# Banded attention: scores as three rounded passes over split queries and keys, projections three units ahead

## What is computed

```python
q = _apply_rope(proj(Wq, bq)); k = _apply_rope(proj(Wk, bk)); v = proj(Wv, bv)   # 16 heads of 64
qb, kb, vb = (y.reshape(b, NH, nb, W, HD) for y in (q, k, v))                    # blocks of W = 128 tokens
kcat = concat([previous block of kb (zeros for the first), kb])                  # 256 keys per block
scores = einsum('bhnqd,bhnkd->bhnqk', qb, kcat) * scale
scores = where(band and valid, scores, -1e30)
ctx = einsum('bhnqk,bhnkd->bhnqd', softmax(scores), vcat)
x = x + merged(ctx) @ Wo.T + bo
```

## Time and profile before

| | us |
|---|---|
| median of 3 runs (1678.68 to 1683.46) | 1678.73 |
| the profiled execution: its time | 1680.55 |
| the profiled execution: its span | 1678.8 |
| busy in the span: TensorE | 1300.5 |
| VectorE | 1008.7 |
| ScalarE | 918.3 |
| GpSimd | 777.6 |
| window stage, from its first to its last operation, about | 57 to 820 |

### The profile page before, as it was taken

The page is one execution under the profiler, slowest core; times in us unless marked ns, Lnnn a source line. Parts: engine busy times, 40 slices in busy tenths (PEclk is TensorE's granted clock), DMA queues, the critical chain, the costliest instruction groups (busy, mean ns, idle before and its releaser), DMA issues. The chain is left out here.

```text
span 1678.8 us, 35216 instructions
## 1 busy us (share of the span) xinstructions
PE 1300.5 (77%) x9684; PEld 1014.9 (60%) x9684; DVE 1008.7 (60%) x3721; ACT 918.3 (55%) x2325; POOL 777.6 (46%) x797
## 2 busy tenths in 40 slices
PE   0699899999999999999641788925988954187891
PEld 0466666666666666666431688912775844177891
DVE  5565566666666656666684445646885877344553
ACT  1377677777776777777541444513765854044450
POOL 4356566666666666656377244510000007634451
PEclk9799999999999999999855898967999975589896
DMA  5799990000000000000311121130000001121115
GB/s 182 135 208 201 207 204 16 0 1 0 1 0 0 1 0 1 0 1 0 101 51 51 53 65 49 62 103 1 1 2 1 0 2 53 48 60 58 57 56 150
DMA packets 129331, 91.55 MB, mean 55 GB/s; under 512 B 9083, under 2 KB 121998, under 8 KB 128960
## 3 DMA queue, kind: packets, MB, share of 16 engines
q1 hardware_dynamic: 118848, 71.32, 20.1%
q0 software_dynamic: 9216, 16.94, 2.9%
q10 hardware_dynamic: 1152, 2.13, 0.4%
HBM read 30.86 MB, written 61.57 MB: 55 GB/s over the span
## 5 line engine op out<-in xcount | busy, mean ns | idle before, releaser
L666 DVE CUSTOM_DVE_ANT_0 sc<-ps,mask 128x256 f32<-128x256 f32 x518 | 199.3, 422 | 280.7 <-PE ps L507 279.6
L787 POOL TENSOR_TENSOR rot<-rot,sin 128x512 f32<-128x512 f32 x132 | 184.4, 1397 | 249.8 <-DVE rot L675 249.8
L598 ACT ACTIVATE sc<-sc,mx 128x256 f32<-128x256 f32 x516 | 256.9, 501 | 20.0 <-DVE mx L666 11.7
L422 POOL DMA_INDIRECT xg<-xw,slot x128 | 123.9, 968 | 287.1 <-DVE slot L284 251.7
L919 POOL DMA_INDIRECT yt<-yo,xt x160 | 160.3, 1002 | 204.8 <-DVE yo L1019 175.6
L606 ACT COPY pT<-pt 128x512 f32<-128x512 f32 x257 | 150.6, 586 | 149.4 <-PE pt L517 138.4
L507 PE MATMUL ps<-K,Q 64*128 64x256 f32 x1036 | 185.5, 434 | 1.7 <-DVE mx L666 1.7
L979 ACT ACTIVATE hT<-ph,b 128x256 f32<-128x256 f32 x320 | 125.7, 477 | 87.7 <-PE ph L942 87.7
L517 PE MATMUL pt<-ident,sc 128*128 128x128 f32 x1028 | 169.8, 288 | 0.0
L530 PE MATMUL po<-pT,V 128*64 128x128 f32 x2048 | 169.3, 286 | 0.0
L960 PE MATMUL py<-w2s,hT 128*128 128x128 f32 x1280 | 162.2, 282 | 1.4 <-ACT hT L979 1.4
(11 more groups left out here) (185 smaller groups left out, 2846.3 us busy)
## 6 DMA issues: line engine op xcount, KB each, us to landing
xg<-zeros SPq DMA_DIRECT2D x76, 520.0 KB, 10.0
xt<-xg SPq DMA_DIRECT2D x80, 130.0 KB, 2.1
got<-yt SPq DMA_DIRECT2D x32, 256.0 KB, 5.0
yt<-yo,xt POOLq DMA_INDIRECT x160, 2.2
x<-in_hidden SPq DMA_DIRECT2D x8, 256.0 KB, 8.3
w<-in_w SPq DMA_DIRECT2D x1, 2048.0 KB, 9.7
xg<-xw,slot POOLq DMA_INDIRECT x128, 2.3
out_x<-x SPq DMA_DIRECT2D x8, 256.0 KB, 4.2
```

Source lines behind the costliest of these rows:

```text
L422: nc.gpsimd.indirect_dma_start(out=rows, out_offset=bass.IndirectOffsetOnAxis(ap=s.slot[:, r, t:t + 1], axis=0), in_=s.xw[:, r, t, :], in_ ...
L598: nc.scalar.activation(sc[:, b, h, :], sc[:, b, h, :], ACT.Exp, scale=-1.0, bias=mx[:, b, h:h + 1], accum_out=ls[:, c % 2, b, h:h + 1]).th ...
L666: nc.vector.tensor_tensor_reduce(sc[:, b, h, :], ps[:, h, 0:2 * P], (mask0 if b == 0 else mask)[:, :], -float(HD) ** -0.5, 3e38, ALU.add, ...
L787: nc.gpsimd.tensor_tensor(rot[:, which, :], rot[:, which, :], s.sin[:, pos(sb)], ALU.mult).then_inc(S["pool"], 1)
```

## The change

In the window stage, Q and K are each kept as two tiles of rounded fp32 (`Qh`, `Ql`, `Kh`, `Kl`): a high part and what is left. A head's scores are three products, high by high, low K by high Q, high K by low Q, summed in PSUM. GpSimd writes its sum back into `lin` (`q_sum`, `k_sum`); ScalarE rounds it into the high tile (`high`, L629 of the changed kernel), and VectorE subtracts that from `lin` into the low tile (`low`, L703), which now counts `q_rdy` or `k_rdy`. For Q, `high` runs behind `read_pt` in b = 2 and `low` behind the maxima in b = 3; for K both run in b = 0 of the next iteration. Projections are three units ahead (`AHEAD = 3`). The first 128 columns of K are copied twice. The experts' outputs are awaited by pairs of superblocks, with 4 semaphores for 8.

```diff
-    nc.gpsimd.memset(s.K[:, :, :], 0.0)
+    for part in s.K:
+        nc.gpsimd.memset(part[:, :, :].bitcast(F32), 0.0)
...
-            sp.dma_start(got[:, k, r, :], parts[k][:, r, :]).then_inc(s.fetched[i], 16)
+            sp.dma_start(got[:, k, r, :], parts[k][:, r, :]).then_inc(s.fetched[i // 2], 16)
...
-    ch.eng.wait_ge(s.fetched[i], 16 * TOPK * nth)
+    ch.eng.wait_ge(s.fetched[i // 2], 32 * TOPK * nth)
...
-            return u, u + 2, (c + 2) % CHUNKS, (sb if c + 2 < CHUNKS else sb + 1)
+            return u, u + AHEAD, (c + AHEAD) % CHUNKS, (sb if c + AHEAD < CHUNKS else sb + 1)
...
-                    ins = nc.tensor.matmul(ps[:, h, 0:2 * P], Q[r, c % QBUF, b * P:(b + 1) * P],
-                                           K[r, c, b * P:(b + 2) * P], start=True, stop=True)
+                    for n, (i, j) in enumerate(((0, 0), (0, 1), (1, 0))):
+                        ins = nc.tensor.matmul(ps[:, h, 0:2 * P], Q[i][r, c % QBUF, b * P:(b + 1) * P],
+                                               K[j][r, c, b * P:(b + 2) * P], start=(n == 0), stop=(n == 2))
...
+            def high(v, c, which):
+
+                act.wait_ge(S["k_sum" if which else "q_sum"], START + v + 1)
+                if which:
+                    act.wait_ge(S["k_prev"], START + v + 1)
+                to = K[0][:, c, P:] if which else Q[0][:, c % QBUF, :]
+                nc.scalar.copy(to, lin[:, which, :]).then_inc(S["k_high" if which else "q_high"], 1)
...
-            for v in range(2):
+            for v in range(AHEAD):
                 read_q(v, v, v0=(v == 0))
                 read_k(v, v, v0=(v == 0))
+                high(v, v, 0)
+                if v < AHEAD - 1:
+                    high(v, v, 1)
...
                         if b == 0:
+                            high(v - 1, (vc - 1) % CHUNKS, 1)
                             read_q(v, vc)
+                        if b == 2:
+                            high(v, vc, 0)
...
+            def low(v, c, which):
+
+                dve.wait_ge(S["k_high" if which else "q_high"], START + v + 1)
+                to, high = (x[:, c, P:] if which else x[:, c % QBUF, :] for x in ((K if which else Q)[1], (K if which else Q)[0]))
+                nc.vector.tensor_tensor(to, lin[:, which, :], high.bitcast(F32), ALU.subtract).then_inc(
+                    S["k_rdy" if which else "q_rdy"], 1)
...
-            for v in range(2):
+            for v in range(AHEAD):
...
+                low(v, v, 0)
+                if v < AHEAD - 1:
+                    low(v, v, 1)
...
+                        if b == 3:
+                            low(v, vc, 0)
                         if b == 0:
+                            low(v - 1, (vc - 1) % CHUNKS, 1)
                             normalise(u - 1, (c - 1) % CHUNKS)
...
-                if which:
-                    pool.wait_ge(S["k_prev"], START + v + 1)
...
-                nc.gpsimd.tensor_tensor(K[:, c, P:] if which else Q[:, c % QBUF, :], lin[:, which, :],
-                                        rot[:, which, :], ALU.add).then_inc(S["k_rdy" if which else "q_rdy"], 1)
+                nc.gpsimd.tensor_tensor(lin[:, which, :], lin[:, which, :], rot[:, which, :], ALU.add).then_inc(
+                    S["k_sum" if which else "q_sum"], 1)
...
-                nc.gpsimd.tensor_copy(K[:, c, 0:P], K[:, c, SB:]).then_inc(S["k_prev"], 1)
+                nc.gpsimd.tensor_copy(K[0][:, c, 0:P], K[0][:, c, SB:])
+                nc.gpsimd.tensor_copy(K[1][:, c, 0:P], K[1][:, c, SB:]).then_inc(S["k_prev"], 1)
```

More of the change, by code:

```diff
@@ L97 @@
     "norm0": NORM + " xT high",
-    "window": "xs xh xl q_ps k_ps v_ps q_sb k_sb v_sb q_sh k_sh q_cos k_cos q_rdy k_rdy "
+    "window": "xs xh xl q_ps k_ps v_ps q_sb k_sb v_sb q_sh k_sh q_cos k_cos q_sum k_sum q_high k_high q_rdy k_rdy "
               "k_prev v_prev s max p t pt pv rs rb r r_sb norm out res chain pool",
@@ L441, in window_stage @@
         xh, xl = (m.sb(n, [P, 2, SB], F32R) for n in ("xh", "xl"))
-        Q = m.sb("Q", [P, QBUF, SB])
+        Q = [m.sb(n, [P, QBUF, SB], F32R) for n in ("Qh", "Ql")]
         K, V, masks, mask = s.K, s.V, s.masks, s.mask
@@ L459, in window_stage @@
         S = s.signals["window"]
+        AHEAD = 3
         swap = [(w + 16) % 32 for w in range(32)]
@@ L484, in project_q @@
                 else:
-                    pe.wait_ge(S["r_sb"], START + v - 2)
+                    pe.wait_ge(S["r_sb"], START + v - AHEAD)
                 project(s.wqh, s.wql, c, sb).then_inc(S["q_ps"], 1)
@@ L535, in turn_sums @@
                 pe.wait_ge(S["rb"], START + u + 1)
-                pe.wait_ge(S["v_sb"], START + u + 3 + CHUNKS)
+                pe.wait_ge(S["v_sb"], START + u + AHEAD + 1 + CHUNKS)
                 for t in range(SB_TILES):
@@ L814, in unit @@
                 if spreads:
-                    spread(v - 2, (c - 2) % CHUNKS)
+                    spread(v - AHEAD, (c - AHEAD) % CHUNKS)
                 rotate(v, c, sb, 1)
             low_x(0)
-            for v in range(2):
+            for v in range(AHEAD):
                 unit(v, v, 0)
@@ L1320, in bass_hybrid @@
         s.put = [m.sem(f"e_put{k}") for k in range(STEP)]
-        s.fetched = [m.sem(f"got{i}") for i in range(NSB)]
+        s.fetched = [m.sem(f"got{i}") for i in range(NSB // 2)]
         s.signals = {stage: {n: m.sem(f"{stage}_{n}") for n in names.split()} for stage, names in SIGNALS.items()}
@@ L1332, in bass_hybrid @@
             s.wq, s.wk = (x[:, :, :].rearrange("p a (b c) -> p (a b) c", c=P) for x in (s.lin, s.rot))
-            s.K = a.sb("K", [P, CHUNKS, P + SB])
+            s.K = [a.sb(n, [P, CHUNKS, P + SB], F32R) for n in ("Kh", "Kl")]
             s.V = a.sb("V", [P, CHUNKS, 1 + SB_TILES, 2, HD])
```

## The result

The changed kernel is slower: 1725.56 us median (1723.16 to 1730.92, 4 runs) against 1680.6 (1678.68 to 1683.46, 4 runs), a ratio of 1.027 (95% interval 1.0239 to 1.0302). Its profiled execution took 1723.16.

A forecast was written before the change was run, and what follows sets the result against it. A ring through VectorE, GpSimd and TensorE was taken to set the window stage's pace. Ring 27, superblocks 8, head 10 and paired reads 4 made +49 on a median of 1678.73: 1730 us, range 1705 to 1760.

The forecast's parts named there:

- the ring: Window stage, VectorE, GpSimd, TensorE, now ScalarE's rounding too: 11.80 us per unit, 0.42 more, +27 us.
- Scores at 0.56: One block's scores on TensorE: three rounded passes, heads side by side, 0.56 us instead of 0.63.
- heads in a row: Rival on TensorE's scores: five products in a row, 0.79 per block, +15, 1745 us; chance 0.20.
- no side by side at all: Rival on TensorE's scores: all six products in a row, 0.91 per block, +22, 1753 us; chance 0.08.
- faster GpSimd: Rival: GpSimd's spread loses 0.3 or 0.4 when VectorE's work shifts, unit 11.58, 1710 us; chance 0.09.
- The signs: Expected in the profile: unit 11.8, VectorE idle about 0.9 before the keys' subtraction, TensorE about 1.2 before the turn.
- the main step: The added wait in the window stage's unit, said to be wrong if the unit is under 11.4 us.
- The second ring: Q's rounding on ScalarE in block 2, waiting for GpSimd's sum: 11.58 us, adding nothing, but a floor.
- Once per superblock: Adding the output to x and rounding x lose their slack: 1.0 per superblock (0.5 to 1.4), +8 us.
- The mask's copy: Once per superblock: a smaller operation that might add time, allowed for within 0.5 to 1.4 us.
- The head: Start of the window stage, three units ahead instead of two: first maximum at 85.4, +10 us.
- Paired reads: Expert outputs awaited in pairs: 2.5 us in the norm stage and 1.4 at the end, together +4 us.

The follow-up runs named there:

- e3: The changed kernel with ScalarE rounding the keys ahead of its read of the transposed probabilities in block 0: 1702.6 us, ratio 1.0110.
- e12: The changed kernel with the keys' rounding ahead of ScalarE's read and the back edges of all four engines' loops hinted: 1681.6 us, ratio 0.9971.
- e5: The kernel before with 16 already satisfied waits per unit added to TensorE's loop: 1687.6 us, ratio 1.0018.
- e9: The kernel before with 56 already satisfied waits per unit added to TensorE's loop: 1715.1 us, ratio 1.0167.
- e4: The changed kernel without the product of low K and high Q, so two passes instead of three: 1700.1 us, ratio 1.0101.
- e7: The changed kernel with the back edge of TensorE's loop hinted: 1710.6 us, ratio 1.0145.
- e10: The changed kernel with the keys rounded ahead of ScalarE's read, projections two units ahead, TensorE's back edge hinted: 1716.1 us, ratio 1.0175.
- e14: The kernel before with the back edges of all four engines' loops hinted: 1677.5 us, ratio 0.9955.

## Why the prediction was right, and where its terms were off

The forecast was 1730 (range 1705 to 1760), the result 1725.6, for the forecast's main reason in kind but not in its sizes: an added wait on the ring through ScalarE and VectorE, little gain from TensorE's shorter scores. That the total came so near is in part luck, as the last paragraph of this section shows.

- **The ring** was right step by step and 0.31 too long: 11.49, not 11.80. Two hand-overs make up nearly all of it. From the read to the next ScalarE operation I took 0.63 from a pair in which the second waits; it is 411.78 - 411.30 = 0.48, the second starting 0.11 before the first ends. From the start of the rounding to that of the subtraction I took 0.62 + 0.14; it is 412.43 - 411.78 = 0.65, so the release costs 0.03. So +7.6 us from plain units instead of +27. That this is the ring e3 shows: taking the rounding off it gives 11.20.
- **Scores at 0.56**: right, and the rivals of heads in a row (0.79) and of no side by side at all (0.91) are out. So is the one of a faster GpSimd: the spread takes 1.07 as against 1.08. The Trainium skill's rule of strict order (TensorE: Matmul & The Clock Gate, Part 3: Packing small matmuls) disagrees with the rows of the boundary above, where head 1's high product starts ahead of head 0's low one.
- **The signs**: TensorE's idle time before the turn was put at 1.2; it is 0.71. VectorE's wait for the rounding was put at about 0.9; it is 0.62. The unit, at 11.49, is only 0.09 above the 11.4 under which the main step would have been wrong.
- **The second ring**, Q's rounding, was put at 11.58 and so at a floor for the unit. e3 and e12 run at 11.20, so that floor was wrong. By the changed kernel's trace it is about 10.4: read to GpSimd's product 3.95 and not 4.23, product and sum 3.00 and not 3.03, the hand-over 0.03 and not 0.10, the rounding 0.53 and not 0.66, two reads 0.95 and not 1.28, and two exponentials, twice, 0.99 and not 1.14.
- **Once per superblock**: adding the output cost 0.60, as forecast. The rounding of x cost nothing. The mask's copy, which I had only allowed for in the range, cost 0.71: it takes 0.33 us, and the next maximum stands another 0.37 idle, waiting for it. Together 1.3 instead of 1.0: 10.5 us instead of 8. e3 takes nearly all of both away by giving VectorE its slack back.
- **The boundaries** were in no term: 11.9 us. I had costed TensorE's added products by time on the array alone, and not as instructions in a loop. e5, e9, e4 and e7 settle that it is TensorE's back edge with a longer body.
- **The head**: +10 was forecast up to the first maximum, and it came 15.2 later. From the stage's first rounding of x on I had 85.4 - 56.94 = 28.5; it took 90.49 - 61.40 = 29.1, two units of 8.5 and 8.8 among it. So the working of the stage was nearly right, though the third unit's part took 7.4 instead of 6.3 and the start before the first read 0.8 less than before. The start of the stage, 4.5 later, was the miss: "zeroing the second K falls into the stage before ... nothing" looked at GpSimd's idle time and not at VectorE, which 3.8 us of it held up; the other 0.65 lies before the norm stage's first operation (19.22 instead of 18.57) and is unexplained. From there to the first spread 1.7 came back.
- **Paired reads**: +4 was forecast, nothing measured.

In sum 27 + 8 + 10 + 4 was forecast, and 7.6 + 10.5 + 11.9 + 13.5, less 2.3, measured in the spans (+41.4; +45 in the medians). The total was close by luck: a term that was not there in the forecast (the boundaries, 11.9) stood in for most of the 19 us by which another was too large (the ring).

## What to carry to other kernels

When a ring of several engines sets the pace, place an added operation in the gap where its engine waits anyway: the same two operations cost 0.29 us a unit behind ScalarE's read and nothing ahead of it. Take hand-overs from two neighbouring rows of which the second doesn't wait for anything else. Count what a change adds to the body of a long unrolled loop, and look at the top of each engine's loop for idle time with no releaser before splitting instructions into more; and look at what a "free" GpSimd operation does to VectorE beside it.

## What the runs showed of the hardware that was not expected

- **Loop back edges.** Without a hint TensorE stood 1.7 to 2.3 us (4.5 the first time) at the top of a loop of 1757 records a superblock, with packets on q8; with 1692 records there were none. ScalarE stood 3.32 behind the first back edge of the kernel before, and 1.90 at a later one of e10, with packets on q14 around it. Hints on all four loops removed the stalls and the packets on both queues (boundary units of 11.19 in e12 and 11.35 in e14).
- **VectorE beside GpSimd.** The same subtraction takes 0.69 alone (keys) and 1.64 beside GpSimd's product and sum of K (queries). The groups of L703 of the changed kernel, from 240 to 840 us:

```profile
L703 DVE TENSOR_TENSOR Ql<-lin,Qh 128x512 fp32r<-128x512 f32 x51 | 83.8, 1643 | 0.0
L703 DVE TENSOR_TENSOR Kl<-lin,Kh 128x512 fp32r<-128x512 f32 x51 | 35.3, 692 | 37.8 <-ACT Kh L629 37.8
```

Queries' subtraction is hidden, so this cost no time here. The Trainium skill (SBUF — State Buffer, Who interferes with whom) says that a VectorE instruction with two inputs in SBUF contends with a GpSimd instruction that reads SBUF; the 1.64 agrees with it. The 4.07 us are another case: one input on VectorE, and a zeroing that only writes. For that the Trainium skill names, in the same section, VectorE operations in its 2-port modes, which GpSimd, when it starts first, blocks for a whole instruction. The 4.07 inside the zeroing's 4.38 fits it; whether this operation ran in such a mode no run shows. That the second copy of K could be zeroed elsewhere, for some 4 us, was not tried.
- **Rounded products on 64 rows** of 256 columns start 0.12 apart, as those on 128 rows do, with two heads side by side.
